# One exp for the four null-key scores of a head, and the inverse-denominator loads issued by GpSimd

## What is computed

```python
xn = layernorm(x)
k, v = split(xn @ Wkv);  q = layernorm(xn, gamma) @ Wq        # q: 16 heads of 64
k, v = concat([null_k, k]), concat([null_v, v])               # 2 null keys in front
q, k = l2norm(q) * q_scale, l2norm(k) * k_scale
attn = softmax(mask(8.0 * q @ k.T))                           # causal, first 64 free
attn_out = (attn @ v) @ Wout
Wq1, Wq2 = quantize(W1), quantize(W2)   # clip(round(W / (mean|W| + eps)), -1, 1)
ffn_out = relu(xn @ Wq1.T + b1) @ Wq2.T + b2
y = x + attn_out + ffn_out
```

## Time and profile before

| | us | share of the span |
|---|---|---|
| median of three runs | 2054.23 | |
| profiled execution | 2046.4 | |
| its span (slowest core) | 2044.9 | 100% |
| TensorE matmul busy | 1554.3 | 76% |
| ScalarE busy | 647.8 | 32% |
| VectorE busy | 469.5 | 23% |
| GpSimd busy | 136.6 | 7% |
| mean granted TensorE clock | 0.764 of 2.4 GHz | |

### The profile page before, as it was taken

The page is one execution under the profiler, slowest core; times in us unless marked ns, Lnnn a source line. Parts: engine busy times, 40 slices in busy tenths (PEclk is TensorE's granted clock), DMA queues, the critical chain, the costliest instruction groups (busy, mean ns, idle before and its releaser), DMA issues.

```text
span 2044.9 us, 20678 instructions; the slowest of 8 cores (2020.2 to 2044.9 us)
## 1 busy us (share of the span) xinstructions
PE 1554.3 (76%) x5609; PEld 577.3 (28%) x5609; DVE 469.5 (23%) x1616; ACT 647.8 (32%) x1315; POOL 136.6 (7%) x201
## 2 busy tenths in 40 slices
PE   0422357777778899999999994299889898988985
PEld 0111112222222223233233321244334343433432
DVE  1344454544343211122212210100110010011000
ACT  0000023342334566677777762012002101200210
POOL 2000000000000010111101110000000000000000
PEclk9666655555567667778798976589779969987998
DMA  4122234443533344454455545511231213123123
GB/s 117 49 55 54 55 104 123 140 130 109 147 108 80 89 103 104 113 114 113 114 119 115 123 108 144 130 52 41 93 113 42 79 57 105 50 86 100 42 82 99
DMA packets 184272, 194.23 MB, mean 95 GB/s; under 512 B 114142, under 2 KB 152288, under 8 KB 183136
## 3 DMA queue, kind: packets, MB, share of 16 engines
q10 hardware_dynamic: 42624, 97.14, 15.7%
q1 hardware_dynamic: 126240, 51.40, 11.2%
q0 software_dynamic: 15296, 44.38, 8.4%
HBM read 139.26 MB, written 29.49 MB: 83 GB/s over the span
## 4 chain that ended last, share of the span: by engine, by line
PE 59%; DMA 19%; DVE 10%; issue 6%; ACT 4%; ACTq 1%; POOL 1%; DVEq 0%; SPq 0%; POOLq 0%
PE psim L1127 11%; PE pwork L863 9%; PE pav L897 8%; PE psim L1151 6%; PE psim L816 6%; PE pwork L1151 5%; PE psim L1042 3%; DMA ktok<-kvT_sb 3%; DMA xbufB<-x 2%; DMA xnTg<-xnt 2%; DVE qtmp L747 2%; DMA wtout<-wqbf 2%; DMA wstage<-W 2%; DVE qhat L762 2%; ACT attnT L829 2%
## 5 line engine op out<-in xcount | busy, mean ns | idle before, releaser
L829 ACT ACTIVATE attnT<-psim,negC 128x512 bf16<-128x512 f32 (+3 forms) x515 | 298.8, 622 | 185.0 <-PE psim L816 69.7
L1142 ACT ACTIVATE h1full<-psim,b_sb 128x512 bf16<-128x512 f32 x128 | 86.7, 687 | 636.0 <-PE psim L1127 566.4
L897 PE MATMUL pav<-attnT,v_sb 128*64 128x512 bf16 (+3 forms) x640 | 274.7, 433 | 12.2 <-DVE outunT L915 12.2
L1127 PE MATMUL psim<-xnTg,W1B 128*128 128x512 bf16 x1024 | 240.6, 379 | 16.4 <-ACT h1full L1142 16.4
L816 PE MATMUL psim<-qhatT,khsT 64*128 64x512 bf16 (+3 forms) x515 | 213.3, 414 | 19.4 <-ACT attnT L829 10.7
L863 PE MATMUL pwork<-attnT,dind 128*2 128x512 bf16 (+3 forms) x640 | 192.6, 469 | 0.0
L1151 PE MATMUL psim<-w2ring,h1full 128*128 128x512 bf16 x512 | 171.8, 421 | 7.9 <-DMA w2ring<-w2qt 7.8
L1151 PE MATMUL pwork<-w2ring,h1full 128*128 128x512 bf16 x512 | 172.7, 422 | 0.0
L518 DVE TENSOR_SCALAR wqbf<-wstage 128x512 bf16<-128x512 f32 x128 | 54.7, 427 | 393.2 <-ACT wstage L505 200.1
L1127 PEld LDWEIGHTS psim<-xnTg,W1B 128*128 128x128 bf16 x1024 | 99.0, 98 | 140.0 <-issue 22.9
L1042 PE MATMUL psim<-invdenT,indic 2*128 2x128 f32 x256 | 70.7, 415 | 73.5 <-issue 56.1
(11 more groups left out here) (141 smaller groups left out, 1264.8 us busy)
## 6 DMA issues: line engine op xcount, KB each, us to landing
wstage<-W ACTq DMA_DIRECT2D x128, 512.0 KB, 4.2
w2ring<-w2qt SPq DMA_DIRECT2D x32, 512.0 KB, 3.5
w2ring<-w2qt ACTq DMA_DIRECT2D x32, 512.0 KB, 3.4
xbufA<-x POOLq DMA_DIRECT2D x16, 512.0 KB, 4.7
w1qt<-wtout POOLq DMA_DIRECT2D x32, 256.0 KB, 3.2
w2qt<-wtout POOLq DMA_DIRECT2D x32, 256.0 KB, 3.2
xbufB<-x POOLq DMA_DIRECT2D x32, 256.0 KB, 3.9
wstage<-Wq ACTq DMA_DIRECT2D x8, 512.0 KB, 4.4
```

The source lines that it names most:

```text
L829: ts_=ts_: s.activation(attnT[:, ts_, c, j0 * 128:j0 * 128 + w], ring_ap2(slot, 0, 128, 0, w), AF.Exp, bias=negC[:, 0:1]),
L897: w=w: t.matmul(pav[po:po + 64, j0 * 128:j0 * 128 + w], v_sb[:, c, :], attnT[:, ts_, c, j0 * 128:j0 * 128 + w], start=(c == 0), stop=False ...
L1127: sp=sp: tt.matmul(PM1[rot][:, 0:TW], W1B[:, c, fc * 128:(fc + 1) * 128], xnTg[:, sp, c, :], start=(c == 0), stop=(c == ND - 1)),
L1142: s.activation(h1full[:, fc, 0:TW], PM1[rot][:, 0:TW], AF.Relu, bias=b1_sb[:, fc:fc + 1]),
```

## The change

Part one: in emit_nulls the four matmuls of a head (two null keys against 128 query rows each) write four column ranges of one ring slot instead of four slots, and one exp of 2x512 reads them, instead of four of 2x128. Part two: the loads of the inverse denominators are issued by GpSimd's queue instead of ScalarE's.

```diff
@@ emit_nulls
+        slot = ring_ctr % NRS
+        ring_ctr += 1
+        t_ns = ring_tok[slot]
         for ib in range(BQ):
-            slot = ring_ctr % NRS
-            ring_ctr += 1
             lqn = qhatT[po:po + 64, bp, cc, ib * 128:(ib + 1) * 128]
-            t_ns = prog.add("tensor", lambda tt, slot=slot, lqn=lqn, po=po:
-                            tt.matmul(
-                ring_ap2(slot, 0, 2, 0, 128), nkhsT[po:po + 64, :], lqn,
-                start=True, stop=True),
-                [t_qT[base + ib], t_kv_done[base + ib], ring_tok[slot]])
-            t_ne = prog.add("scalar", lambda s, slot=slot, ts_=ts_, ib=ib:
-                            s.activation(
-                attnTn[:, ts_, ib * 128:(ib + 1) * 128],
-                ring_ap2(slot, 0, 2, 0, 128), AF.Exp,
-                bias=negC[0:2, 0:1]), [t_ns, t_negC, attnTn_free[ts_]])
-            ring_tok[slot] = t_ne
-            hd["t_nes"].append(t_ne)
+            t_ns = prog.add("tensor", lambda tt, slot=slot, lqn=lqn, po=po,
+                            ib=ib: tt.matmul(
+                ring_ap2(slot, 0, 2, ib * 128, 128), nkhsT[po:po + 64, :],
+                lqn, start=True, stop=True),
+                [t_qT[base + ib], t_kv_done[base + ib], t_ns])
+        t_ne = prog.add("scalar", lambda s, slot=slot, ts_=ts_:
+                        s.activation(
+            attnTn[:, ts_, :], ring_ap2(slot, 0, 2, 0, BW), AF.Exp,
+            bias=negC[0:2, 0:1]), [t_ns, t_negC, attnTn_free[ts_]])
+        ring_tok[slot] = t_ne
+        hd["t_nes"].append(t_ne)
@@ den_steps
-                ds["ivl"] = prog.dma("scalar", lambda g, j=j, spp=spp:
+                ds["ivl"] = prog.dma("gpsimd", lambda g, j=j, spp=spp:
```

## The result

The changed kernel takes 1969.71 us (median of 10 runs) against 2052.92 us of the kernel before on the same chip, a ratio of the means of 0.9611 (95% interval 0.9586 to 0.9636), some 80 us. Forecast were 2009 us and -45 us. The direction, the place and the order of the mechanism were right, and the size was nearly twice what I gave.

The account below looks back on a forecast made before the run. Engines waiting for each other bound the first two attention blocks, TensorE the last two. Terms -48 - 8 + 11 + 0 = -45 us took 2046.4 to 2001.4 us, scaled by 1.0038 to 2009 us; range 1958 to 2052.

Parts of the forecast that it names:

- What bounds, and the wait in front of the null matmuls: First two attention blocks: engines waiting for each other bound; 79.9 us of TensorE idle before null matmuls, released by ScalarE's exps.
- Its size in the first two blocks: Null-key change, 250 to 740 us: 60% of 79.9 us of waits goes, -48 us, between -10 and -80.
- less than 40: Expected sign before 740 us: TensorE's waits in front of scores grow, but to less than 40 us.
- signs of being wrong: Score waits growing as much as null waits fall, exposed loads over 4 us, or granted clock before 740 us leaving 0.6.
- The last two blocks: Attention, 740 to 1260 us: TensorE is full, so only 8 of 14.1 us of null waits goes, between 0 and 14.
- a rival, for the first two blocks: Clock there rises with shorter gaps, second block's to 0.75: -100 us in all, 1954 us; chance 0.12.
- ScalarE's saving: Merged null exp saves 0.47 us a head, 30 us over 64 heads; inside the 60% first, worth nothing in last blocks.
- The loads: Output phase: 12 exposed inverse-denominator loads cost +0.9 us each on GpSimd's queue (+0.5 start, +0.4 landing), +11 us.
- The 0 for the first load behind Wout: Output phase start: first load queued behind Wout on GpSimd could bring -4 or +6 us; taken as 0.
- The rival of the slow loads: Output phase: 12 exposed loads at upper price, +28 us, and earlier clock fall; +23 us in all, 2077 us; chance 0.10.
- its +5 us: Slow-loads rival, output phase: clock falls one load earlier in a later group, 12.2 us replacing some 7, +5 us.
- The rival of the moved wait: Attention phase: the stall moves from null matmuls to the next scores; -4 us in all, 2050 us; chance 0.16.

Follow-up runs that it names:

- part one: One slot and one exp per head for the null keys, inverse-denominator loads left on ScalarE's queue, against the kernel before: ratio 0.9588 (0.9538 to 0.9638).

## Why the prediction was right, and where not

**What bounds, and the wait in front of the null matmuls: right, and shown.** The kernel with one slot and the old waits is as slow as before; the one with four exps and one slot as fast as part one.

**Its size in the first two blocks: right as a sum, by two errors that cancel.** Forecast -48 us from 60% of 79.9; measured -53. That the sum came so close is luck. Of the first block's -27 us, 10 are less busy time and 17 less idle time (length less busy: 65.9 to 49.1 us); of the second's -26, 14 and 12. So of the 76 us of waits that went in front of the null matmuls only 29 stayed gone, 38% and not 60%; a higher clock and denser null matmuls, which I had at nothing, gave the other 24. Score waits of 28 us fit the "less than 40". I had not named the transposes that wait for VectorE (12 to 33 us), which are now the longest wait in those blocks. One of my signs of being wrong came true: the granted clock of those blocks left 0.6 (0.615 and 0.647), upwards.

**The last two blocks: the step that failed.** I counted 8 of 14.1 us of waits and took TensorE's busy time as fixed. Measured were -36 us. In the third block, part one against before, mean of the cores: idle time -8.4 us (15.5 to 7.1), the null matmuls 11.4 to 7.0 us busy because four without a wait between them overlap, the sums behind them 53.9 to 46.8 us at a higher clock, scores and value products together 4.3 us less. That this is not chance is shown by the kernel with the old waits: a clock of 0.826 and 11.4 us of null matmuls, as before (0.830), while the kernels with one slot and no such waits have 0.852 to 0.882. But the waits are not the whole account of the clock: with the sums first and four slots they were gone from this block as well, and the clock was 0.778. What sets it there is not shown. I had the clock only in a rival, for the first two blocks, and priced it as all or nothing. It came as a part in every block: 0.580 to 0.615, 0.599 to 0.647, 0.830 to 0.875.

**ScalarE's saving: wrong in the loop.** I held it to be inside the 60% in the first blocks. One exp with four slots: 1.0019. The exp took 668 ns, not 629, so the saving was 0.43 us a head and not 0.47; that changes nothing.

**The loads: right, and a little dear.** +0.56 us each instead of +0.9: my +0.5 for the start held, my +0.4 for the landing came from 256 KB stores and did not carry over to 8 KB loads (2.0 us to landing, and the matmul followed the issue as soon as on ScalarE's queue). For the whole part two the two ratios give 5 us each, no more than their intervals allow to tell from nothing, the waits 4.9 to 6.7; 11 were forecast. The 0 for the first load behind Wout held too: from the issue of the Wout load to the first spread it was 48.3 us before and 48.0 after, in the mean of the cores.

**The rival of the slow loads** had one true half: the clock falls at these waits. It had fallen there before the change as well, so part two could hardly make it worse, and its +5 us did not show. What I missed is that the same trace said how much these waits already cost: not 15 us, but 15 plus three stretches of 41, 38 and 38 us at the 1.2 GHz level. That was nearly as large as the change's own gain, and it lay outside the change. Another wait lies there untouched: from the issue of the Wout load to the first spread TensorE has next to nothing to do, 45 to 48 us in every version measured here.

**The rival of the moved wait** was half right. It put the return in front of the scores, and that was 15 us (13 to 28); with VectorE's two places 48 of the 76 us did come back. It was wrong in what follows from that: the work passed over and the clock made the blocks shorter all the same.

## What to carry to other kernels

When a small side job takes slots of the ring that paces the main loop, count whose release each of its operations waits for, and what ready work stands behind it: here the waits that its four slots brought, and not the exps saved, were worth 4%. A wait of TensorE is not worth its own length alone. Look at the granted clock in the stretches after it: in the output phase 9.5 us of waits in the midst of dense work cost some 56 us, while 7.3 us at its start cost about their own length. To hide a load that waits for its own buffer's readers, alternate the buffers by load before thinking about the queue that issues it.

## What the runs showed of the hardware

Four null matmuls in a row without a semaphore of ScalarE between them took 7.0 us of busy time per 16 heads in the third block instead of 11.4 (part one against before). GpSimd's queue landed an 8 KB load in 2.0 us, and the first matmul that reads a load started 2.25 us after the issue, on ScalarE's queue 2.26; only the start was later, 0.70 us after the release instead of 0.14. In the first group of the changed kernel, on its slowest core, two waits of 1.96 and 1.98 us with 6.5 us of dense work between them stood before the fall of TensorE's clock from the 2.4 to the 1.2 GHz level, and the low level then lasted while it was busy 4.9 to 6.0 of each 6 us. Why the third block had a clock of 0.778 with the sums first and four slots, although TensorE waited there as little as in the faster kernels, stays open.
